# Key transposes of a gated cross-attention kernel in 64-row blocks, in the array tiling of the matmuls around them

## What is computed

```python
def xattn(q, k, v, Wq, Wk, Wv, Wo, bo, g):      # q, k, v: (32, 64 channels, 512 positions); k = v = context
    qh = einsum('bcn,oc->bon', q, Wq).reshape(b, 8, 64, -1)     # 8 heads of 64
    kh = einsum('bcn,oc->bon', k, Wk).reshape(b, 8, 64, -1)
    vh = einsum('bcn,oc->bon', v, Wv).reshape(b, 8, 64, -1)
    qh = softmax(qh, axis=-2) * 64 ** -0.5      # over the 64 of a head
    kh = softmax(kh, axis=-1)                   # over the positions
    context = einsum('bhdn,bhen->bhde', kh, vh)
    out = einsum('bhde,bhdn->bhen', context, qh).reshape(b, 512, -1)
    out = einsum('bcn,oc->bon', out, Wo) + bo
    return out / max(norm(out, axis=1), 1e-12) * g * 8
x = x + tanh(g_xattn) * xattn(layernorm(x), ctx, ctx, ...)
x = x + tanh(g_ffn) * ffn(layernorm(x))         # gate, up, down from 4-bit weights, SiLU
```

## Time and profile before

| | us |
|---|---|
| median of 3 runs | 786.22 |
| the profiled execution | 788.89 |
| its span, first to last instruction | 787.1 |
| attention, until the first feed-forward matmul | 497.1 |
| one steady step | 26.1 |
| PE busy, of the span | 732.0 |
| DVE busy | 594.7 |
| ACT busy | 436.3 |

### The profile page before, as it was taken

The page is one execution under the profiler, slowest core; times in us unless marked ns, Lnnn a source line. Parts: engine busy times, 40 slices in busy tenths (PEclk is TensorE's granted clock), DMA queues, the critical chain, the costliest instruction groups (busy, mean ns, idle before and its releaser), DMA issues. The chain is left out here.

```text
span 787.1 us, 13752 instructions
## 1 busy us (share of the span) xinstructions
PE 732.0 (93%) x4551; PEld 395.1 (50%) x4551; DVE 594.7 (76%) x806; ACT 436.3 (55%) x764; POOL 179.5 (23%) x317
## 2 busy tenths in 40 slices
PE   4789999999999999999999754799999999999997
PEld 3445554565456545654565331254555455554555
DVE  6356878887888788778876463699988878877885
ACT  3657776677667767776776421354443344445333
POOL 5221222222222222222241112112121111111221
PEclk9999999999999999999999956799999999999999
DMA  3003303330233012202200000200001000100101
GB/s 102 28 5 84 81 13 85 85 85 11 80 82 84 19 58 69 71 16 61 70 20 7 4 4 1 75 1 0 1 2 40 15 0 13 40 0 0 40 13 54
DMA packets 29195, 29.89 MB, mean 38 GB/s; under 512 B 18628, under 2 KB 18756, under 8 KB 29036
## 3 DMA queue, kind: packets, MB, share of 16 engines
q1 hardware_dynamic: 26972, 28.85, 13.3%
q10 hardware_dynamic: 2192, 0.66, 0.3%
HBM read 23.49 MB, written 4.23 MB: 35 GB/s over the span
## 5 line engine op out<-in xcount | busy, mean ns | idle before, releaser
L1303 DVE SCALAR_TENSOR_TENSOR acc<-ffn_bank,scale_T,acc 128x512 f32<-128x512 f32 (+1 forms) x264 | 186.6, 747 | 39.6 <-PE ffn_bank L1256 34.1
L1255 PE MATMUL ffn_bank<-ek,w_gu 128*128 (+3 forms) x352 | 137.8, 392 | 3.0 <-PEq L90 1.8
L1256 PE MATMUL ffn_bank<-ekT,w_gu 128*128 (+3 forms) x352 | 134.1, 381 | 0.0
L987 DVE TENSOR_TENSOR eq<-eq,pair 128x1024 f32<-128x1024 f32 x64 | 78.1, 1221 | 65.8 <-PE pair L743 65.8
L1163 POOL TENSOR_TENSOR in_lo<-inter,in_hi 128x512 fp32r<-128x512 f32 (+1 forms) x44 | 56.4, 1283 | 229.8 <-ACT in_hi L1202 229.8
L1195 ACT ACTIVATE act_gate<-acc 128x512 f32<-128x512 f32 (+1 forms) x44 | 27.7, 631 | 144.3 <-DVE acc L1303 144.3
L484 ACT ACTIVATE ek<-pair,kneg 128x512 f32<-128x512 f32 x128 | 86.7, 686 | 8.2 <-DVE kneg L982 7.8
L1272 PE MATMUL ffn_bank<-wd_hi,in_hi 128*128 128x512 f32 (+1 forms) x176 | 86.7, 531 | 0.4 <-DVE wd_lo L1336 0.4
L979 DVE TENSOR_REDUCE qmax<-pair 128x16 f32<-128x1024 f32 x64 | 77.6, 1212 | 12.4 <-PE pair L625 12.2
L1272 PE MATMUL ffn_bank<-wd_lo,in_hi 128*128 128x512 f32 (+1 forms) x176 | 86.7, 531 | 0.0
L493 ACT ACTIVATE eq<-pair 128x1024 f32<-128x1024 f32 x64 | 65.7, 1026 | 30.5 <-PE pair L763 30.5
(11 more groups left out here) (138 smaller groups left out, 1147.0 us busy)
## 6 DMA issues: line engine op xcount, KB each, us to landing
xall<-in_x SPq DMA_DIRECT2D x16, 256.0 KB, 2.7
ctx_raw<-in_ctx SPq DMA_DIRECT2D x16, 256.0 KB, 2.9
out_x<-xall SPq DMA_DIRECT2D x16, 256.0 KB, 2.0
zero<-zeros_plus SPq DMA_DIRECT2D x8, 344.0 KB, 4.3
packed<-in_L_ffn_gate_qweight SPq DMA_DIRECT2D x4, 688.0 KB
packed<-in_L_ffn_up_qweight SPq DMA_DIRECT2D x4, 688.0 KB
packed<-in_L_ffn_down_qweight SPq DMA_DIRECT2D x10, 256.0 KB
d_scale<-in_L_ffn_down_scales SPq DMA_DIRECT2D x1, 1408.0 KB, 6.2
```

Of the source, the lines that this page charges most:

```text
L987: dve.tensor_tensor(e, e, dve_pair[:, :, :], ALU.mult).then_inc(q_norm, 1)
L1255: pe.matmul(gu_bank[job % 4][0:w, :], lhsT, xT_hi[:, g, rows], start=True, stop=False)
L1256: pe.matmul(gu_bank[job % 4][0:w, :], lhsT, xT_lo[:, g, rows], start=False, stop=True).then_inc(gu_mm, 1)
L1303: dve.scalar_tensor_tensor(out=acc[0:w, it % 3, m, :], in0=gu_bank[job % 4][0:w, :], scalar=scale_T[0:w, it, 4 * m + g:4 * m + g + 1], in1 ...
```

## The change

k_transposed(t) makes sixteen transposes in place of eight. Each takes 64 rows of ek (one half of the partitions) and 128 positions, and has a 64x64 piece of the identity as its moving operand, so 64 columns stream in place of 128. The two halves e = 0 and 1 follow each other and write to the two banks of act_pair. ekT therefore has another layout: the half e outside, then element and channel tile; context() reads it back by a strided pattern of 4 x 2 x 64 elements. spread_inverse_norm takes 64 rows of its operands. The wait for the last key exponential (k_exp) stands before the last pair of q_logits(0) in place of before k_transposed(0), which gets a wait on pool_consts, a semaphore that is long past that value.

```diff
@@ context
-                        last = pe.matmul(small[0][half(b), :], ctxT[:, t, half(b)], ekT[:, t, b, :],
-                                         start=(t == 0), stop=(t == NT - 1))
+                        heads = ekT[:, t, :, b * OT * DH:(b + 1) * OT * DH].rearrange("n e (t d) -> n t e d", d=DH)
+                        last = pe.matmul(small[0][half(b), :].rearrange("c (t e d) -> c t e d", t=OT, e=2),
+                                         ctxT[:, t, half(b)], heads, start=(t == 0), stop=(t == NT - 1))
@@ q_logits
+                    if t == 0:
+                        pe.wait_ge(k_exp, 8 * p + 8)
                     for b in range(2):
                         last = pe.matmul(k_pair[:, b, :], minus_spread[half(b), t, :], qmax_rows[half(b), :],
                                          start=False, stop=True)
@@ k_transposed
-                    if t == 0:
-                        pe.wait_ge(k_exp, 8 * p + 8)
-                    else:
+                    pe.wait_ge(pool_consts, 2)
+                    if t > 0:
                         pe.wait_ge(kt_evac, 4 * p + t)
-                    for b in range(2):
-                        for ot in range(OT):
-                            last = pe.transpose(act_pair[:, b, ot * P:(ot + 1) * P], ek[:, b, ot, t * P:(t + 1) * P],
-                                                ident[:, :])
+                    for slot in range(2 * OT):
+                        b, ot = divmod(slot, OT)
+                        for e in range(2):
+                            last = pe.transpose(act_pair[:, e, slot * DH:(slot + 1) * DH],
+                                                ek[half(e), b, ot, t * P:(t + 1) * P], ident[half(e), half(e)])
                     last.then_inc(kt_mm, 1)
@@ spread_inverse_norm
-                    pe.matmul(small[0][:, :], spread_batch[:, :], rn_rows[:, :], start=True, stop=True).then_inc(rn_mm, 1)
+                    pe.matmul(small[0][:, :], spread_batch[0:C, :], rn_rows[0:C, :], start=True, stop=True).then_inc(rn_mm, 1)
```

## The result

The changed kernel takes 775.66 us, the median of 4 runs (775.3 to 776.3), where the kernel before, run beside it, takes 786.26. The ratio is 0.9852, with a 95% interval from 0.9835 to 0.9869. Forecast were 774.2 us and a range from 769.5 to 781.5. The profiled executions are 788.89 us before and 776.33 after, a difference of 12.6; 11.95 of it are there already when the feed-forward stage begins (497.13 us before, 485.18 after). One execution of the kernel before, among those beside the runs of the half exponential, took 1437.8 us and stands in no ratio.

What follows compares the result with a forecast made beforehand. PE sets the step until tile 1, then ACT's exponential handover binds at 2.32 us a cycle; of 2.65 us a step off PE, 0.75 comes out. 16 x 0.75 = 12.0 off 786.2 gives 774.2 us, range 769.5 to 781.5.

Steps and rivals of the forecast that it cites:

- PE's saving would not come out whole: Loop step: PE would have 42 us less over 16 steps, but only 12.0 would reach the end, as ACT binds.
- 2.65 us a step off PE: PE's work per step: 4 x 0.40 from transposes, 4 x 0.15 and 3 x 0.20 from tiling changes, less 0.15.
- The 0.20 that I put down to the change of tiling behind a block: From the end of the transposes' streaming to L743: 0.20 us lost, three such losses a step to go.
- The 0.15 ahead of a block: From q_logits' last pair to the transposes: 0.15 us lost to a tiling change, four to go, one to come.
- The cycle of 2.32: PE-ACT handover of k_pair: 2.32 us from load to load, seen in step 0, which PE cannot shorten.
- Two chains 0.1 behind ACT: Inverse norm's transfers hidden by 0.1 us; DVE's maximum lets t_logits(1) go at 12.05, PE arriving at 12.13.
- The overlap of the halves: Transposes: two 64-row halves load and stream side by side, 0.058 us a pair, a block 0.47 instead of 0.87.
- the second rival: Halves do not overlap or tiling gaps stay: block 0.90, gain 0.4 us a step, 779.8 us; chance 0.14.
- The gain per step: Steady step: 0.72 us sooner at k_logits(0), 0.80 with an earlier exponential of tile 1; 0.75 taken.
- The sum of 16 steps: Whole loop: 16 x 0.75 = 12.0 us off, step 0 counted like the others.
- The strided read: context()'s read of ekT (L691, 3.9 us a step): costed at nothing; doubled it would give 836 us.
- PE idle by 1.5 us of a step: Sign expected if right: a step of 25.35 us with PE idle some 1.5 us of it.

Runs made afterwards that it cites:

- half exponential: Changed kernel with ACT computing the query exponential for only one of two batch elements in steps 4 to 13: 775.13 us, ratio 0.9847.
- extra change of tiling: Changed kernel plus one overwritten 128x128 transpose ahead of a block: 774.45 us with it at t = 1 and 3, 780.98 us at t = 0 alone.
- both edits: Changed kernel with half the query exponential left out in steps 4 to 13 and spread_inverse_norm moved behind q_logits(3): 766.31 us, ratio 0.9742.
- late norm: Changed kernel with spread_inverse_norm moved behind q_logits(3): 774.82 us, ratio 0.9855.
- halves in turn: Changed kernel with each block's eight lower-half transposes first, then the eight upper-half ones: 780.52 us, ratio 0.9909.
- the repeated run: Second run of the changed kernel with the inverse norm spread from 128 rows again: 777.83 us, ratio 0.9882.

## Why the prediction was right

All times are from the first matmul of q_logits(0), 235.99 in the step shown.

| step of the prediction | forecast | measured |
|---|---|---|
| a block, to the next matmul of its tiling | 0.47 and the next load | 0.55 |
| q_logits(0)'s last pair to the transposes | 0.23 | 0.23 |
| q_logits(1) | 2.42 | 2.44 |
| exponential of tile 1 | 3.65 (3.57 with overlap) | 3.57 |
| load of q_logits(2) | 4.73 | 4.65 |
| inverse norm | 6.48 | 6.48 |
| last normalise | 7.25 | 7.26 |
| load of k_logits(0) | 9.37 | 9.28 |
| t_logits(1) | 12.05 | 12.07 |
| length of a step | 25.35 | 25.34 |

- **That PE's saving would not come out whole** held, and it is the step on which the result hung. Shown by the extra change of tiling that is free at t = 1 and 3 and costs its full price at t = 0.
- **The 2.65 us a step off PE** were too much, and it did no harm only because ACT hides that term. Between q_logits(1) and q_logits(2) PE needs 239.91 + 0.34 - 238.43 = 1.82 by itself (and takes 1.82 in the kernel with both edits), where I had 1.63 and where it was 2.38: 0.56 less in each of the later rounds and not 0.75. With the 0.38 of the first that makes about 2.1, of which 0.82 come out. The 0.20 that I put down to the change of tiling behind a block holds the 0.11 of L744's load, and that is exposed behind the 64-row block as well: from L744 to L762 still 0.34 (238.09 to 238.43), where a pair takes 0.23. The 0.15 ahead of a block turned out as 0.09 (0.32 to 0.23 from start to start).
- **The cycle of 2.32** from step 0 held to 0.01 in all later rounds.
- **Two chains 0.1 behind ACT** held nearly. The halved exponential and the late norm give 0.06 and 0.01 apart and 0.83 together. But DVE is level with PE at t_logits(1) and not 0.1 ahead of it, as 12.05 against 12.13 had said: its load waits for DVE for 0.84 to 0.88, before for 0.84. A longer wait there was one of my signs of being wrong, and it came, at 0.02 in the mean. It takes next to nothing from the gain of a step.
- **The overlap of the halves** held. A slot of two is 0.062 rather than 0.058, which put q_logits(1) 0.02 late and nothing at the end. With the halves in turn the kernel is at 780.52, where the second rival had 779.8. Part of that nearness is luck: the step gained 0.54 where the rival had 0.4, and the kernel before stood at 788.44 beside it, so 7.9 us were gained and not 6.4. What a second bank adds to the overlap stays open.
- **The gain per step** was 0.82, where I took 0.75 out of 0.72 to 0.80. What I had wrong is what holds the exponential of tile 1. I took ACT's copies to follow without a gap and the ctxT copy to end at 3.65. But the 1.02 to the first copy was a wait for PE's block: all forty such copies between 130 and 385 us of the kernel before start 0.04 after the end of the block's record, so the shorter block moves the copy as well: it follows at 0.92, the ctxT copy ends at 3.56, and PE's q_logits(1) at 2.44 + 1.13 = 3.57 sets the start. The 0.08 are the difference between my 0.72 and 0.80; the 0.75 between them was a choice, not a reading.
- **The sum of 16 steps** gives 13.1 by the measured step, and 12.6 arrived between the profiled executions, 10.6 between the medians. The medians of before themselves lie between 786.2 and 788.4 in the sets that were run, which is most of this difference. My 12.0 came from too little a step (0.75); that it lies between the two measured differences is in part owed to stretches outside the steps, and to that extent luck.
- **The strided read**: L691 has a median of 592 ns before and L692 has 592 after, so it costs nothing. Rows by line, before and after:

```profile
L691 PE MATMUL small<-ekT,ctxT x176: 592/592/643, 130.2 to 396.4; 128*64 128x512 f32 x176
```

```profile
L692 PE MATMUL small<-ekT,ctxT x168: 592/592/644, 130.6 to 385.3; 128*64 128x512 f32 x168
```

- **PE idle by 1.5 us of a step** was wrong as I put it. The window shows 25.30 - 24.84 = 0.46. The waits stand on the weight loads, and add up to 0.54 + 0.25 + 0.18 + 0.47 = 1.44 there, while the records of the matmuls before them run on past their streaming and hide most of it. That is why a PE at 98% of a step could be an engine that waits.

Open is what the moved wait for k_exp does by itself: it wasn't tried alone. In the changed kernel no row between 130 and 400 us charges idle time of PE to it. Open is too whether the halves overlap because they use other rows or because they write to another bank. Open too is whether ACT's handover can be made shorter without leaving work out.

## What to carry to other kernels

Before adding up what an edit saves on the busiest engine, look for a buffer that one engine writes, another reads and the first overwrites. The time from load to load of such a handover is a floor, and a stretch of the same trace in which the engine has less to do shows it. Where several chains end within 0.1 us, probe with dummy work and with work left out, singly and together: one edit alone may show nothing, and it may also leave in place the chain that it was meant to remove. Judge edits inside a loop by the length of its steps, not by the total, when the clock of other stretches varies.

## What the runs showed of the hardware

- Transposes in the 64-row tiling go at 0.062 us for a pair of 64x64 blocks when the two row halves (and with them the two banks) alternate, 1.8 times the rate of the 0.109 us for a 128x128 one. In turn they take 0.06 each, with a few pairs at the seam.
- A single 128x128 transpose between a 64-row pair and a 64-row block delays the block by 0.35 us, both changes of tiling and the transpose included, and the block itself takes 0.06 more (0.65 in place of 0.59 at t = 0).
- A 64-row matmul of 512 columns ahead of a 64-row pair: the pair's row starts 0.10 us after it (242.47 to 242.57) and is 0.63 long in place of 0.50, so it ends 0.73 after the start of the single one. With 128 rows the pair starts 0.43 after it (243.43 to 243.86 in the repeated run) and ends 0.93 after it.
- Reading the moving operand in runs of 64 elements costs nothing: 592 ns either way.
- A copy on ACT started 0.04 us after the record of the PE block that it reads ended (244.28 to 244.32), an exponential 0.04 to 0.05 after that of its last pair (237.08 to 237.13).
